# The weights and first keys and values of a third attention, moved into the expert loop of the layer before it

## What is computed

```python
x = x + tanh(g_ffn[1]) * L1_ffn(layernorm(x))
x = x + tanh(g_xattn[2]) * L2_xattn(layernorm(x), ctx_1024, mask)

def L1_ffn(x):                       # 8 experts, 256 -> 1024 -> 256
    p = softmax(x @ gate_w.T); e = argmax(p)
    return (relu(x @ w1[e] + b1[e]) @ w2[e] + b2[e]) * p[e]

def L2_xattn(query, value, mask):    # 16 heads of 64
    q = einsum('btd,dnh->btnh', query, Wq) + bq
    k = einsum('bsd,dnh->bsnh', value, Wk) + bk
    v = einsum('bsd,dnh->bsnh', value, Wv) + bv
    probs = softmax(einsum('bsnh,btnh->bnts', k, q) / 8 + (1 - mask) * -10000)
    return einsum('btnh,nhd->btd', einsum('bnts,bsnh->btnh', probs, v), Wo) + bo
```

## Time and profile before

| | us |
|---|---|
| median of 3 runs | 1620.52 |
| lowest, highest | 1617.87, 2092.66 |
| profiled execution | 1625.24 |
| its span, first to last instruction | 1623.5 |

### The profile page before, as it was taken

One profiled execution on the slowest core, in us unless ns is written; L12 is line 12 of the kernel. 1 busy time (PEld: TensorE's weight loads), 2 busy tenths in 40 slices (PEclk: granted clock), 3 DMA queues, 4 the chain that ended last, 5 costly groups with the idle time before them and its releaser, 6 DMA issues. The chain is left out here.

```text
span 1623.5 us, 31277 instructions
## 1 busy us (share of the span) xinstructions
PE 1387.9 (85%) x10534; PEld 1139.3 (70%) x10534; DVE 944.5 (58%) x2315; ACT 648.7 (40%) x1297; POOL 422.7 (26%) x577
## 2 busy tenths in 40 slices
PE   8999878899999958999999999999999998301588
PEld 5888545778799946888888879688888896300245
DVE  4888755665422246777777756522222264488887
ACT  3666552501444412333333333344545532421277
POOL 1000000021222201222222231255555644421131
PEclk8999998998899978999999997799999999655699
DMA  3000200972111125111111102022222344621001
GB/s 101 21 22 17 74 22 1 338 211 78 37 34 40 30 65 181 50 50 48 48 42 38 42 16 77 20 75 79 78 79 82 87 160 144 158 17 11 0 14 40
DMA packets 106560, 110.71 MB, mean 68 GB/s; under 512 B 36161, under 2 KB 92369, under 8 KB 106321
## 3 DMA queue, kind: packets, MB, share of 16 engines
q1 hardware_dynamic: 90544, 75.11, 15.1%
q0 software_dynamic: 11136, 28.93, 6.3%
q10 hardware_dynamic: 4768, 5.25, 1.1%
HBM read 87.38 MB, written 20.71 MB: 67 GB/s over the span
## 5 line engine op out<-in xcount | busy, mean ns | idle before, releaser
L3588 PEld LDWEIGHTS L2f_bank<-L2f_xT,L2f_w_tile 128*128 128x128 f32 x1264 | 152.0, 192 | 12.0 <-ACT L2f_xT L3652 3.7
L3588 PE MATMUL L2f_bank<-L2f_xT,L2f_w_tile 128*128 128x128 f32 x1264 | 155.9, 277 | 3.7 <-ACT L2f_xT L3652 3.2
L790 POOL TENSOR_TENSOR L2x_probs<-L2x_probs,L2x_inv_sum 128x512 f32<-128x512 f32 x64 | 66.2, 1055 | 267.6 <-DVE L2x_inv_sum L1067 267.6
L3702 DVE TENSOR_TENSOR L2f_hT<-L2f_gate_h,L2f_bank 128x256 f32<-128x256 f32 x79 | 33.3, 421 | 170.9 <-ACT L2f_gate_h L3659 160.3
L3511 POOL DMA_INDIRECT L2f_y_rows<-L2f_xn,L2f_put_row x79 | 78.0, 987 | 84.2 <-DVE L2f_xn L3718 69.9
L3605 PE MATMUL L2f_bank<-L2f_w_down,L2f_hT 128*128 x316 | 83.6, 387 | 16.3 <-DVE L2f_hT L3702 15.8
L3503 POOL DMA_INDIRECT L2f_rows<-L2f_x_rows,L2f_take_row x79 | 76.8, 972 | 45.4 <-issue 22.6
L3588 PEld LDWEIGHTS L1f_bank<-L1f_xT,L1f_w_tile 128*128 128x128 f32 x736 | 85.6, 192 | 1.1
L3588 PE MATMUL L1f_bank<-L1f_xT,L1f_w_tile 128*128 128x128 f32 x736 | 85.9, 275 | 0.0
L3646 ACT COPY L2f_w_tile<-L2f_w_up 128x1024 f32 x79 | 82.9, 1049 | 6.8 <-issue 4.3
L3605 PE MATMUL L1f_bank<-L1f_w_down,L1f_hT 128*128 x368 | 83.1, 379 | 0.0
(11 more groups left out here) (666 smaller groups left out, 3272.6 us busy)
## 6 DMA issues: line engine op xcount, KB each, us to landing
L1f_w_up<-in_L_ffn_w SPq DMA_DIRECT2D x16, 512.0 KB, 8.4
L1f_w_down<-in_L_ffn_w SPq DMA_DIRECT2D x16, 512.0 KB, 9.6
L2f_got<-L2f_y_rows SPq DMA_DIRECT2D x16, 512.0 KB, 4.4
L2f_w_up<-in_L_ffn_gate_w SPq DMA_DIRECT2D x16, 256.0 KB, 2.9
L2f_w_up<-in_L_ffn_up_w SPq DMA_DIRECT2D x16, 256.0 KB, 3.1
L2f_w_down<-in_L_ffn_down_w SPq DMA_DIRECT2D x16, 256.0 KB, 3.4
x<-in_x SPq DMA_DIRECT2D x4, 512.0 KB, 7.4
L0x_cT<-in_ctx_turned SPq DMA_DIRECT2D x16, 128.0 KB, 2.1
```

Source lines behind the costliest of these rows:

```text
L790: nc.gpsimd.tensor_tensor(probs[c][:, :, :], probs[c][:, :, :], inv_sum[:, c, :][:, :, None].to_broadcast([P, 4, P]), ALU.mult).then_inc(s ...
L3588: x = nc.tensor.matmul(products(j, m), w_tile[j][:, at:at + P], xT[j][:, k * P:(k + 1) * P], start=(k == 0), stop=(k == KT - 1))
L3702: nc.vector.tensor_tensor(hT[j][:, 0:F], gate_h[j][:, 0:F], bank[2 + j][:, F:2 * F], ALU.mult).then_inc(q["h"], 1)
```

## The change

It does four things.

1. One block of memory, `shared`, is made once for the second and third layer. In it lie, in turn, the second layer's turned rows, first expert weights and weight tiles, the third attention's weights, its keys and values, the third layer's second expert weights and several of its tiles.
2. `WideStart` holds the third attention's query, key, value and output weights, the context of batches 0 and 1, the key bias and two buffers each for keys and values. In the block of the second layer's tile loop and additions, SP waits until the last weight tile is copied (`w_tile` = S), then asks for the context of two batches, the key bias, and the key, value and query weights; behind the loads of the gathered rows it asks for the output weights.
3. Behind its tile loop TensorE makes the keys and the values of batches 0 and 1, in the eight PSUM banks of that loop, and ScalarE copies them out, ahead of the table load that ends its part.
4. `wide_attention` no longer makes or copies keys and values for batches 0 and 1. Batch 0 starts with T, Q0, Q1 and both groups of scores; the warm-up products ahead of K0 are gone. The counts behind which the engines wait are worked out anew (`fill_no`), and two banks are chosen otherwise (`bank_of`). SP asks for the inputs of batches 2 and 3 without waiting for the fronts of batches 0 and 1.

```diff
+SHARED_DOWN = 4 * KT * 1024
+SHARED_TILE = 2 * SHARED_DOWN
+SHARED = SHARED_TILE + 4 * 1024
+class WideStart:
...
+    def load_first(self, sp):
+        ins = self.core.ins
+        sp.dma_start(self.cT[:, :], turned_ctx(ins, 0, 2)).then_inc(self.sems["ctx_bk"], 16)
+        sp.dma_start(self.bk[:, :], ins[L2_X["bk"]].rearrange("n h -> (n h)").rearrange("(t p) -> p t", p=P),
+                     allow_slow_non_contiguous=True).then_inc(self.sems["ctx_bk"], 16)
+        for name in ("wk", "wv", "wq"):
+            self.load(sp, name)
...
+    def take_keys(self, act, bank, b, half):
+        act.wait_ge(self.sems["k"], 2 * b + half + 1)
+        for i in range(4):
+            t = 4 * half + i
+            self.core.nc.scalar.activation(self.kT[b][:, t, :], bank[:, i * P:(i + 1) * P], ACT.Identity,
+                                           bias=self.bk[:, t:t + 1])
...
@@ routed_experts, TensorE, behind over_tiles
+            if following:
+                pe.wait_ge(q["h"], S)
+                pe.wait_ge(q["h_act"], S)
+                pe.wait_ge(following.sems["ctx_bk"], 32)
+                for b in range(2):
+                    if b == 0:
+                        pe.wait_ge(following.sems["w_k"], 16 * KT)
+                    for half in range(2):
+                        following.keys(pe, bank[2 + 2 * b + half], b, half)
+                pe.wait_ge(following.sems["w_v"], 16 * KT)
+                pe.wait_ge(q["y"], S)
+                for b in range(2):
+                    for half in range(2):
+                        following.values(pe, bank[(0 if b == 0 else 6) + half], b, half)
@@ routed_experts, SyncE
+            if following:
+                sp.wait_ge(q["w_tile"], S)
+                following.load_first(sp)
             for j in range(4):
                 sp.wait_ge(q[f"stored{j}"], 16 * len(range(j, S, 4)))
...
+            if following:
+                following.load_last(sp)
@@ wide_attention, SyncE
             def body(j, b):
-                sp.wait_ge(s["filled"], (b - 2) * NF + NF)
-                settle(sp, s["passed"])
+                if not isinstance(b, int):
+                    sp.wait_ge(s["filled"], fill_no(b - 2, NF - 1))
+                    settle(sp, s["passed"])
@@ wide_attention, GpSimd
-            for k in range(KT):
-                pool.dma_start(wq[:, k, :], w2d("wq")[k * P:(k + 1) * P, :]).then_inc(s["w_q"], 16)
@@ wide_attention, TensorE, front
+                if done(b, f):
+                    return
@@ wide_attention, TensorE, start of batch 0
-            for f in range(NF):
-                if f == 0:
-                    stay_warm(core, out_bank, 1)
-                if fills[f] == "Q0":
-                    stay_warm(core, out_bank, 2)
-                    pe.wait_ge(s["w_q"], 16 * KT)
-                if fills[f] == "K0":
-                    stay_warm(core, out_bank, 2)
-                    pe.wait_ge(s["w_k"], 16 * KT)
...
+            stay_warm(core, out_bank, 1)
+            front(0, 0, fills.index("T"))
+            stay_warm(core, out_bank, 2)
+            pe.wait_ge(early["w_q"], 16 * KT)
+            front(0, 0, fills.index("Q0"))
+            front(0, 0, fills.index("Q1"))
+            scores(0, 0, 0)
+            scores(0, 0, 1)
@@ flamingo_stack
+        def layers1_2():
+            with ExitStack() as both:
+                core.shared = core.sbuf_in(both)("shared", [P, SHARED])
+                start = WideStart(core, both)
+                with_experts(lambda ahead: bidirectional_attention(core, ahead), L1_EXPERTS, start)
+                with_experts(lambda ahead: wide_attention(core, ahead, start), L2_EXPERTS)
```

More of the change, by code:

```diff
@@ L680, with wide_attention @@
 L2_MASK = dict(compare=1.0, times=800.0, op=ALU.subtract, diag=100.0)
-def wide_attention(core, ahead):
+def wide_attention(core, ahead, start):
     nc, ins = core.nc, core.ins
@@ L696, in wide_attention @@
         sb = core.sbuf_in(ctx)
-        wq = sb(f"{tag}_wq", [P, KT, E])
-        wk = sb(f"{tag}_wk", [P, KT, E])
-        wv = sb(f"{tag}_wv", [P, KT, E])
-        wo = sb(f"{tag}_wo", [P, KTL, D])
+        wq, wk, wv, wo, kT, v = start.wq, start.wk, start.wv, start.wo, start.kT, start.v
+        early = start.sems
+        core.sems.extend(early.values())
         bo = sb(f"{tag}_bo", [P, D])
@@ L713, in wide_attention @@
         qT = [sb(f"{tag}_qT{j}", [P, KTL, P]) for j in range(2)]
-        kT = [sb(f"{tag}_kT{j}", [P, KTL, P]) for j in range(2)]
-        v = [sb(f"{tag}_v{j}", [P, E]) for j in range(2)]
         top = sb(f"{tag}_top", [P, 2, 4])
@@ L729, in wide_attention, with done, fill_no, bank_of @@
             "bv_wo", "bv_row", "gated_bias", "x_biased"])
+        def done(b, f):
+            return isinstance(b, int) and b < 2 and fills[f][0] in "KV"
+        def fill_no(b, f, kinds="TQKV"):
+            mine = [kind for kind in fills if kind[0] in kinds]
+            first = [kind for kind in mine if kind[0] not in "KV"]
+            upto = [kind for kind in fills[:f + 1] if kind[0] in kinds]
+            if isinstance(b, int) and b < 2:
+                return b * len(first) + len([kind for kind in upto if kind[0] not in "KV"])
+            return b * len(mine) - 2 * (len(mine) - len(first)) + len(upto)
         def evicted(eng, b, f):
             if by_dve[f]:
-                after(eng, s["evicted_dve"], b * ND + sum(by_dve[:f + 1]))
+                after(eng, s["evicted_dve"], fill_no(b, f, "QK"))
             else:
-                after(eng, s["evicted_act"], b * NA + f + 1 - sum(by_dve[:f + 1]))
-        def w2d(name):
-            return ins[L2_X[name]].rearrange("d n h -> d (n h)")
+                after(eng, s["evicted_act"], fill_no(b, f, "TV"))
+        def bank_of(j, b, f):
+            if isinstance(b, int) and b < 2 and f == 3:
+                return front_bank[b]
+            return front_bank[(j * NF + f) % 2]
+        USED_BY = {(0, 3): (0, 0), (1, 0): (0, 1), (1, 1): (0, 3), (1, 3): (1, 0), (2, 0): (1, 1), (2, 1): (1, 3)}
         block = ctx.enter_context(nc.Block())
@@ L773, in body @@
                 ahead.part(sp, b)
-            with sp.Fori(1, B // 2) as i:
+            for j in range(2):
+                body(j, 2 + j)
+            with sp.Fori(2, B // 2) as i:
                 for j in range(2):
@@ L868, in weighted @@
             def weighted(j, b, r):
-                if r == 0:
-                    evicted(pe, b, fills.index("V0"))
-                else:
-                    evicted(pe, b, fills.index("V1"))
+                if not done(b, fills.index("V0")):
+                    evicted(pe, b, fills.index(f"V{r}"))
                 pe.wait_ge(s["pT_out"], b * 4 + (2 * r + 2))
@@ L1022, in take @@
             def take(j, b, f):
-                src = front_bank[(j * NF + f) % 2]
+                if done(b, f):
+                    return
+                src = bank_of(j, b, f)
                 kind = fills[f]
@@ L3008, in __init__ @@
         self.gated = spec["gated"]
-        self.w_up = sb(f"{tag}_w_up", [P, E * KT * F * (2 if self.gated else 1)])
-        self.w_down = sb(f"{tag}_w_down", [P, E * (F // P) * D])
+        up, down = E * KT * F * (2 if self.gated else 1), E * (F // P) * D
+        if self.gated:
+            self.w_up = sb(f"{tag}_w_up", [P, up])
+            self.w_down = core.shared[:, SHARED_DOWN:SHARED_DOWN + down]
+        else:
+            self.w_up = core.shared[:, 0:up]
+            self.w_down = sb(f"{tag}_w_down", [P, down])
         self.down_part = E * (F // P) * D // B
@@ L3692, in _ @@
                     shared_result(act, b)
+            if following:
+                for b in range(2):
+                    for half in range(2):
+                        following.take_keys(act, bank[2 + 2 * b + half], b, half)
+                for b in range(2):
+                    for half in range(2):
+                        following.take_values(act, bank[(0 if b == 0 else 6) + half], b, half)
             nc.scalar.preload_act_table(ACT.Sqrt)
```

126 lines of the change are left out of this document (83 added, 43 removed).

## The result

| | before | changed |
|---|---|---|
| median, 8 executions each, us | 1623.05 | 1612.26 |
| profiled execution, us | 1625.24 | 1612.2 |
| its span, us | 1623.5 | 1610.5 |
| mean granted clock of TensorE | 0.917 | 0.922 |

The account below looks back on a forecast made before the run. TensorE was taken as the bound from batch 2's transposition in the third attention on; its move from 658.99 to 646.3 us gave 12.7 us, taken off the 1620.52 median for 1607.8 us, range 1602.9 to 1615.5.

Parts of the forecast that it names:

- What the end follows: Third attention: TensorE bounds from batch 2's transposition on, so the program's end moves by as much as that instruction, 12.7 us.
- T2: TensorE's transposition for batch 2 in the third attention, forecast to start at 646.3 us instead of 658.99.
- The early loads cost nothing: End of second layer: 3.4 MB asked for at 571.9 us take 14.3 us, in by about 586, before TensorE is free.
- Rival 3: SP's queue at the second layer's end: weights delay the gathered rows, 15.3 us lost, 1623.1 us; chance 0.05.
- Keys and values beside the additions: Border: TensorE's 15.6 us of products lie wholly beside DVE's additions, nothing to spare, cost 0; ScalarE ends at 607.3.
- Rival 2: Border: ScalarE closes the block, its table load holding it another 1.28 us; gain 11.5, 1609.0 us; chance 0.1.
- The first query products at full clock: Third attention's start: no wait for weights, both query halves at 1.95 us each from 613.49; 3.5 us more if not.
- Bias loads: Third attention's start: the last small bias load lands 6.0 us after its start, at 616.1; cost 0, or up to 0.8.
- Gain at the bias sum: DVE's bias sum in the third attention starts at 624.1 us instead of 632.06, 8.0 us gained.
- The chain behind it: DVE's work from the bias sum to batch 2's transposition: gain grows from 8.0 to 12.7 us.
- Rival 1: Third attention: only the first part's 8.0 us stay, the rest comes back as waiting; 1612.5 us; chance 0.2.
- A fall of the clock ahead of T2: Doubt: TensorE, idle 1.5 us from 644.8 to 646.3, might fall to half clock, some 2 us lost.

Follow-up runs that it names:

- loads late: Changed kernel with the early loads asked for behind the waits for the stored rows, directly ahead of the gathered rows: border 30.15 us against 18.77.
- keys made three times: Changed kernel with the keys of both batches made twice more ahead of the ones that count: border 31.31 us against 18.77.
- the kernels between: Kernel before with shared memory alone, then also loads early, then also keys and values of batch 0: T2 at 49.08, 44.22 and 40.40 us.

## Why the prediction was right

Point by point, times from the attention's first product where nothing else is said.

- **What the end follows.** Right within the attention: behind T2 both kernels take 307.9 us of it. That the two profiled spans differ by 13.0, close to the 12.7 forecast, is in part luck: the stages elsewhere differ by 2.87, -3.8 and 1.7 us, and add up to 0.8. By the medians the gain is 10.8, and of the 4.5 us by which 1612.26 lies above the forecast, 2.5 are the median it started from (1620.52 of three runs, 1623.05 of eight).
- **The early loads cost nothing.** Right. 3.4 MB were estimated at 238 GB/s, 14.3 us; the burst from 574.79 to about 587 is some 12. They had some 5 us to spare. Rival 3 (weights ahead of the gathered rows) is false where the loads stand, and its mechanism is real 21 us later on the queue: with loads late the border loses 11.4 us, most of what the change gains.
- **Keys and values beside the additions.** Right that they cost nothing; "with nothing to spare" was wrong. 15.6 us was eight times a row of 1.95, but such a row's modelled end overlaps the next product. Back to back, the starts of ScalarE's copies lie 1.79 us apart for keys and 1.72 for values, and all eight take 14.2 (592.40 to 606.57). That and the shorter last copy (0.58 for 0.68) make the margin 1.74 us, and keys made three times show that it is real. Rival 2 (ScalarE closes the block) is false with it.
- **The first query products at full clock.** Right in size (3.73 us for both halves, 3.9 predicted, starting at 4.90 rather than 5.02), for a reason that was not the predicted one: I had the clock fall before the block, and it fell at its start (below). The warm-up products brought it back in time.
- **Bias loads.** Predicted to land in 6.0 us, just in time; they took 2.5. Of the 6.0, 3.64 was the issue itself; that takes 0.69 now. It changed nothing, as the copy waits for TensorE.
- **Gain at the bias sum.** 8.0 predicted, 23.59 - 15.28 = 8.3 measured.
- **The chain behind it.** The next group 20.4 predicted, 20.07 measured; T2 37.8 predicted, 36.71 measured. The term mis-sized is the 7.0 us from the query copy of batch 1 to its second half out of TensorE. It was taken whole from the row of before, where that half ran at the lower clock for 3.14 us; now the clock came up in it, and it took 2.55. That is 0.6 of the 1.1 us; 0.3 are the start, the rest copies. The prediction had named this as a gain in its list of doubts; of the scores ahead of it, which it named too, it didn't come true: they still ran at the lower clock (2.08).
- **Rival 1, the start alone.** False: the gain is 8.3 at the bias sum and 13.8 at T2, and the kernels between show where it grows: 40.40 to 36.71 for the keys and values of batch 1 alone.
- **A fall of the clock ahead of T2**, some 2 us: it didn't come. TensorE waits 1.42 us there, and the clock is 1.00 from 648 on.

Split by the kernels, the 13.8 us are 1.4 with the shared memory, which by the rows is the clock's moment and not the memory, 4.9 from the early loads (49.08 to 44.22), 3.8 from batch 0's keys and values and 3.7 from batch 1's. Each of these carries the 1 to 2 us, and the last some 2.4, by which T2 moves with the clock. Three executions of the changed kernel and two kernels that are alike from the first product on show how: the clock came back to 2.4 GHz 3.2, 3.4, 3.9, 5.1 and 5.1 us behind the first product, and T2 came at 36.15, 36.30, 36.71, 37.52 and 37.54.

## What to carry to other kernels

An engine that is idle at a barrier takes work that doesn't depend on the chain there for nothing, up to the end of the engine that closes the block (here 1.74 us of margin) and not one us further (12.55 of 14.29 us counted); the margin is read from the ends of all engines, and products priced back to back, not by a row's duration. Where a load is asked for on a queue matters more than that it is early: the same loads 21 us later, in front of others, took back 11.4 of the 13.8 us. When TensorE's work is taken out of a stretch, look at what VectorE's row now holds and where it waits: one call moved into such a wait shortened the stretch by another 3.7 us.

## What I had not expected of the hardware

The granted clock, in stretches of 1.5 us of the changed kernel, TensorE having been idle from 606.57 to 611.33 (columns as in the earlier trace rows):

```profile
607.50:609.00 1.50, 0.00 (x0) 0.00 (x0) 1.50 (x5) 0.99 (x1) 0.00 (x0) 1.00 0.82 238
609.00:610.50 1.50, 0.00 (x0) 0.00 (x0) 1.15 (x4) 0.00 (x0) 0.00 (x0) 1.00 0.82 268
610.50:612.00 1.50, 0.67 (x2) 0.30 (x2) 0.64 (x6) 0.00 (x0) 0.00 (x0) 0.95 0.97 342
612.00:613.50 1.50, 1.07 (x3) 0.22 (x2) 1.24 (x7) 0.22 (x1) 0.00 (x0) 0.50 0.44 104
613.50:615.00 1.50, 1.50 (x4) 0.94 (x4) 0.35 (x2) 0.97 (x2) 0.00 (x0) 0.50 0.84 6
615.00:616.50 1.50, 1.50 (x6) 0.65 (x5) 0.00 (x0) 0.69 (x1) 0.00 (x0) 0.91 0.47 66
```

The clock stayed at 2.4 GHz through 4.75 us without a product, and fell to 1.2 GHz when TensorE had begun to work again. Before, in the same place, it fell within 2.8 us of the last product (0.78 in 591 to 592.5). The other two executions of the changed kernel show 1.00 for at least 4.3 and for 5.3 us of theirs, and 0.50 right behind. With keys three times and with loads late it fell 1.6 us into the next work, 4.6 and 5.1 us behind the last product. So the fall came at anything from 2 to over 5 us behind the last product, in three of these cases into the next work, and a term that hangs on the clock behind a wait of a few us is worth the difference of the two levels for a product or two: here 1 to 2 us at T2.
